# Padding each expert's rows to 64 instead of 128: 36 routed tiles in place of 39, the last four made of two experts' half tiles

## What is computed

```python
logits = x @ wg.T; probs = softmax(logits)            # 8 experts
top_w, top_idx = top_k(probs, 2); top_w /= sum(top_w) # two experts a row
for e in range(8):
    h = silu(x @ ex_gate[e].T) * (x @ ex_up[e].T)     # 256 -> 512
    out += h @ ex_down[e].T * comb[:, e:e+1]          # 512 -> 256
out += shared_mlp(x)                                  # the same form, every row
```

## Time and profile before

| | us |
|---|---|
| median of 3 runs | 375.55 (375.23 to 375.87) |
| profiled execution: span from first to last instruction | 371.5 |
| median less that span | 4.05 |
| TensorE matmul busy | 361.5 (97%) |
| VectorE busy | 280.9 (76%) |
| ScalarE busy | 217.7 (59%) |
| GpSimd busy | 197.4 (53%) |

### The profile page before, as it was taken

How to read it: one execution, slowest core, us unless ns; L and a number is a source line. 1 busy time by engine, 2 the same in 40 slices (tenths; PEclk the granted TensorE clock), 3 DMA queues, 4 the chain that set the end, 5 groups by cost and what they waited for, 6 DMA issues and landing times.

```text
span 371.5 us, 12942 instructions
## 1 busy us (share of the span) xinstructions
PE 361.5 (97%) x4978; PEld 314.9 (85%) x4983; DVE 280.9 (76%) x566; ACT 217.7 (59%) x457; POOL 197.4 (53%) x193
## 2 busy tenths in 40 slices
PE   8989998999999989999999999999999999999996
PEld 5546555788888879899999999999999999999995
DVE  6996388999999985679986887776778685555543
ACT  5688667687777855647357656565565634333222
POOL 2000003977888776122274687878677666674250
PEclk9999999999999999999999999999999999999999
DMA  7953031000198008989434465665757686665543
GB/s 262 379 78 48 2 131 41 2 4 30 41 380 151 30 31 311 347 305 250 109 91 90 112 114 91 106 111 87 118 99 94 106 104 89 104 113 76 71 58 114
DMA packets 53043, 45.35 MB, mean 122 GB/s; under 512 B 31524, under 2 KB 46996, under 8 KB 52856
## 3 DMA queue, kind: packets, MB, share of 16 engines
q1 hardware_dynamic: 43048, 32.09, 31.3%
q0 software_dynamic: 7488, 10.27, 19.0%
q10 hardware_dynamic: 2448, 2.18, 2.2%
HBM read 27.60 MB, written 10.49 MB: 103 GB/s over the span
## 4 chain that ended last, share of the span: by engine, by line
PE 69%; POOL 12%; DVE 7%; issue 5%; ACT 4%; DMA 1%; ACTq 0%; POOLq 0%; DVEq 0%
PE ps L1638 37%; PE ps L1656 18%; PE ps L1420 7%; POOL tmp L558 2%; POOL tmp L579 2%; PE ps L1406 2%; POOL tmp L562 2%; POOL tmp L577 2%; POOL wx L567 2%; POOL h2s L583 2%; DVE st L942 1%; DMA tmp<-in_decay_tables 1%; DVE tmp L959 1%; PE ps L1541 1%; ACT tmp L734 1%
## 5 line engine op out<-in xcount | busy, mean ns | idle before, releaser
L1638 PE MATMUL ps<-tmp,wx 128*128 128x128 bf16 x1776 | 105.5, 219 | 0.0
L1638 PEld LDWEIGHTS ps<-tmp,wx 128*128 (+1 forms) x1776 | 102.2, 98 | 0.9 <-issue 0.2
L615 POOL DMA_INDIRECT out<-tmp,dk x39 | 69.2, 1775 | 39.5 <-SPq L519 35.2
L862 ACT ACTIVATE tmp<-tmp 128x512 bf16<-128x512 f32 x55 | 34.6, 629 | 81.3 <-PE ps L1656 61.2
L1656 PE MATMUL ps<-wx,tmp 128*128 (+1 forms) x660 | 80.8, 273 | 0.2 <-DVE tmp L1267 0.2
L1656 PEld LDWEIGHTS ps<-wx,tmp 128*128 128x128 bf16 x660 | 62.2, 98 | 7.0 <-DVE tmp L1267 0.5
L1261 DVE TENSOR_TENSOR tmp<-ps,tmp 128x512 f32<-128x512 f32 x55 | 37.9, 689 | 36.0 <-PE ps L1638 31.3
L610 POOL DMA_INDIRECT tmp<-h2rows,src_i x39 | 43.5, 1116 | 16.7 <-issue 10.7
L1638 PE MATMUL ps<-w_hl,wx 128*128 128x128 bf16 x864 | 51.3, 219 | 0.5 <-ACT tmp L851 0.5
L1638 PEld LDWEIGHTS ps<-w_hl,wx 128*128 (+1 forms) x864 | 49.6, 98 | 1.1 <-issue 0.6
L1267 DVE TENSOR_TENSOR tmp<-tmp 128x512 bf16<-128x512 f32 x55 | 38.3, 696 | 10.7 <-ACT tmp L862 10.6
(11 more groups left out here) (196 smaller groups left out, 554.8 us busy)
## 6 DMA issues: line engine op xcount, KB each, us to landing
wx<-in_wexp SPq DMA_DIRECT2D x26, 512.0 KB, 5.2
xres<-in_x SPq DMA_DIRECT2D x4, 512.0 KB, 6.8
h2rows<-h2s ACTq DMA_DIRECT2D x16, 128.0 KB, 3.8
out<-h2s SPq DMA_DIRECT2D x12, 128.0 KB
h2s<-in_wmod SPq DMA_DIRECT2D x1, 1024.0 KB, 9.3
wx<-decay_rows SPq DMA_DIRECT2D x16, 64.0 KB
modr<-mod_rows SPq DMA_DIRECT2D x1, 1024.0 KB, 4.6
wx<-in_wqkvu SPq DMA_DIRECT2D x1, 768.0 KB, 7.0
```

What stands on the lines that cost most here:

```text
L615: e.indirect_dma_start(t["out"], bass.IndirectOffsetOnAxis(ap=dst_i[:, j:j + 1], axis=0), yb[(NA + j) % 2], None, compute_op=ALU.add).then ...
L862: e.activation(hs[p][:, 0:FF], hf[p], ACT.Copy).then_inc(s["inner_high"], 1)
L1638: ins = e.matmul(half(bank, m * P), weight(at_, weights(part, w) + k * FF + m * P, P), xT[f % NXT][:, (2 * a + k) * P:(2 * a + k + 1) * P] ...
```

## The change

- Each expert has as many full tiles of 128 as fit, plus one when over 64 rows are left; 1 to 64 left rows are a half. While fewer than 32 tiles are taken, a half gets a tile of its own; behind tile 32 two halves share one. So 32 full tiles are followed by 4 paired ones (PAIRS), 36 in all. The last paired tile has one half only.
- A paired tile makes gate and up with 64 moving columns for each half and its own expert's weights, and down once for each half, over all 128 stationary columns, into its own 256 columns of the bank. Its result is taken in two instructions of 64 partitions. It is added in two adds of 64 rows (the last in one): ADDS has 32 + 2 x 3 + 1 = 39 entries, as before.
- The adds of paired tiles are not asked of SyncE: GpSimd itself waits for the result and for both adds before.
- There are 4 result buffers (NY) in place of 2.
- The routing chain has 15 more links: 13 (with tiles_end, which moves forward) ahead of the marks, 2 more among those of iteration 8; a further instruction that is no link makes dst_upper. The weights' splits follow each other every 3 or 4 tiles instead of every 4.

```diff
+NFULL, NPAIR = TOP * NT, NE // 2
+NG = NFULL + NPAIR
-NG = TOP * NT + NE - 1
+PLACES = [*range(NG)]
+PAIRS = [j for j in range(NG) if PLACES[j] >= NFULL]
+ADDS = [(j, h) for j in range(NG) for h in ((0, 1) if j in PAIRS[:-1] else (0,) if j in PAIRS else (None,))]
+ASKED = [u for u in range(len(ADDS)) if ADDS[u][1] is None and (u == 0 or ADDS[u - 1][1] is None)]
+NY = 4
+SPLIT_FROM = (-1, 2, 6, 9, 13, 16, 20)
+        yb += [woutg[:].rearrange("p b k n -> p (b k n)")[:, (2 + i) * D:(3 + i) * D] for i in range(NY - 2)]
...
+        def halves(f):
+            return (0, 1) if f - NA in PAIRS[:-1] else (0,)
+        def experts_of(j):
+            return min(2 * PLACES[j] // 7 + 1, NE) if PLACES[j] < NFULL else NE
+        def added(eng, u):
+            wait(eng, s_added[u % 2], 16 * (u // 2 + 1) if u >= 0 else 0)
+        def last_add(j):
+            return max(u for u in range(len(ADDS)) if ADDS[u][0] == j) if j >= 0 else -1
...
-        PIECES_AT.update({NA - 1 + 4 * (x - 1) + q: ((x, q),) for x in range(1, NE) for q in range(NPIECE)})
-        ROUTING_AT = {4: 13, 5: 2, 6: 6, 7: 7, 8: 5, 9: 5, 10: 4, 11: 2}
+        PIECES_AT.update({NA + at_ + q: ((x + 1, q),) for x, at_ in enumerate(SPLIT_FROM) for q in range(NPIECE)})
+        ROUTING_AT = {4: 15, 5: 13, 6: 6, 7: 7, 8: 7, 9: 5, 10: 5, 11: 2}
...
             for f in range(NA + 6, NF):
-                if f - NA > 5:
-                    allow_add(f - NA - 6)
+                j = f - NA
+                while allowed < len(ASKED) and ADDS[ASKED[allowed]][0] <= (j - 6 if j - 6 < PAIRS[0] else j - 8):
+                    allow_add(ASKED[allowed])
+                    allowed += 1
                 turn_rows(f)
...
+            def add_rows(u):
+                j, h = ADDS[u]
+                if u in ASKED:
+                    e.wait_ge(s["may_add"], ASKED.index(u) + 1)
+                else:
+                    e.wait_ge(s["result_made"], j + 1)
+                    added(e, u - 2)
+                    added(e, u - 1)
+                rows = slice(0, P) if h is None else slice(h * HP2, (h + 1) * HP2)
+                to = dst_upper[0:HP2, j:j + 1] if h else dst_i[0:rows.stop, j:j + 1]
+                e.indirect_dma_start(t["out"], bass.IndirectOffsetOnAxis(ap=to, axis=0),
+                                     yb[j % NY][rows], None, compute_op=ALU.add).then_inc(s_added[u % 2], 16)
...
-                yield link(e.tensor_scalar(left, counts, float(P - 1), None, ALU.add))
+                yield link(e.tensor_scalar(left, counts, float(HP2 - 1), None, ALU.add))
                 yield link(e.tensor_scalar(tiles, left, -P, None, ALU.bitwise_and))
+                yield link(e.tensor_scalar(odd, left, HP2, HP2.bit_length() - 1, ALU.bitwise_and, ALU.logical_shift_right))
...
+                yield link(e.tensor_tensor(tiles_ahead, ahead, odd.unsqueeze(1).to_broadcast([P, NE, NE]), ALU.mult))
+                yield link(e.tensor_reduce(odd_at, tiles_ahead, AX.X, ALU.add))
+                yield link(e.tensor_reduce(total, tiles, AX.X, ALU.add))
+                yield link(e.tensor_scalar(cap, total, 0.5, float(NFULL * HP2), ALU.mult, ALU.add))
+                yield link(e.tensor_scalar(reach, odd_at, float(HP2), total, ALU.mult, ALU.add))
+                yield link(e.tensor_scalar(reach, reach, cap, total, ALU.min, ALU.max))
+                yield link(e.scalar_tensor_tensor(out=half_at, in0=odd_at, scalar=float(HP2), in1=reach, op0=ALU.mult, op1=ALU.add))
+                yield link(e.tensor_tensor(tiles_end, base, tiles, ALU.add))
+                yield link(e.tensor_tensor(jump, half_at, tiles_end, ALU.subtract))
+                ranks = half(FREE_BANK, 0, NT * NE).rearrange("p (t e) -> p t e", t=NT)
+                yield link(e.tensor_tensor(over, ranks, tiles.unsqueeze(1).to_broadcast([P, NT, NE]), ALU.is_ge))
+                yield link(e.tensor_tensor(over, over, jump.unsqueeze(1).to_broadcast([P, NT, NE]), ALU.mult))
+                yield link(e.tensor_tensor(pos, ranks, base.unsqueeze(1).to_broadcast([P, NT, NE]), ALU.add))
+                yield link(e.tensor_tensor(pos, pos, over, ALU.add))
...
-                    wait(e, s_added[j % 2], 16 * (j // 2))
+                    added(e, last_add(j - NY))
...
+                    for h in halves(f):
+                        rows = slice(h * HP2, (h + 1) * HP2) if paired(f) else slice(0, P)
+                        ins = e.scalar_tensor_tensor(out=yb[j % NY][rows], in0=ps[rows, DOWN_BANKS[f % 2], h * D:(h + 1) * D],
+                                                     scalar=slot_w[rows, j:j + 1], in1=gates[f % 2][rows], op0=ALU.mult, op1=ALU.mult)
+                    ins.then_inc(s["result_made"], 1)
...
+                for h in halves(f):
+                    e.reg_load(slot_reg, slot_of[0:1, 2 * j + h:2 * j + h + 1])
...
+                width = HP2 if paired(f) else P
+                for h, at_ in enumerate(homes):
+                    for m in range(KF):
+                        addresses(at_, [weights(part, w) + k * FF + m * P + LAST_COLUMN for k in range(KD) for w in range(2)])
+                        for n in range(3 * KD):
+                            k, (a, w) = n // 3, PASSES[n % 3]
+                            row = (2 * a + k) * P + h * HP2
+                            ins = e.matmul(half(bank, m * P + h * HP2, width), weight(at_, weights(part, w) + k * FF + m * P, P),
+                                           xT[f % NXT][:, row:row + width], start=n == 0, stop=n == 3 * KD - 1)
...
+                for h, at_ in enumerate(homes):
+                    for n in range(3 * KF):
...
+                        ins = e.matmul(half(DOWN_BANKS[p], h * D, D), hs[p][:, (KF * a + k) * P:(KF * a + k + 1) * P],
+                                       wx[:, off:off + D] if second else weight(at_, weights(2, w) + k * D, D),
+                                       start=n == 0, stop=n == 3 * KF - 1)
```

The two further links are in the chain that finds each half's expert:

```diff
+                yield link(e.scalar_tensor_tensor(out=odd_rank, in0=rank, scalar=-float(NE), in1=odd, op0=ALU.add, op1=ALU.mult))
                 yield link(e.tensor_scalar(passed, tiles_end, tile_col, None, ALU.is_le))
+                yield link(e.scalar_tensor_tensor(out=odd_rank, in0=half_at, scalar=tile_col, in1=odd_rank, op0=ALU.is_equal, op1=ALU.mult))
+                yield link(e.tensor_tensor(passed, passed, odd_rank, ALU.add))
```

More of the change, by code:

```diff
@@ L222, in build @@
         place_i, none_i, dst_i = (of_slots[:, i * NG:(i + 1) * NG].bitcast(u32) for i in range(2, 5))
+        dst_upper = of_slots[:, 5 * NG:6 * NG].bitcast(u32)
         tiles_end, base = (route(NE) for _ in range(2))
-        left, tiles = (route(NE, i32) for _ in range(2))
+        left, tiles, odd = (route(NE, i32) for _ in range(3))
+        odd_at, reach, half_at, jump, odd_rank, total, cap = (route(n) for n in (NE, NE, NE, NE, NE, 1, 1))
+        over = pick
         spare = at_tmp(5796, NG)
@@ L646, in _ @@
                 if j == 0:
-                    e.wait_ge(s["rows_found"], 2)
+                    e.wait_ge(s["rows_found"], 3)
                     e.wait_ge(s["x1_stored"], 16 * (B + 1))
                     e.wait_ge(s["base_stored"], 16 * NA)
-                add_rows(j)
+                for u in range(len(ADDS)):
+                    if ADDS[u][0] == j:
+                        add_rows(u)
         @block.scalar
@@ L1246, in routing @@
                 yield e.tensor_tensor(dst_i, none_i, src_i[:], ALU.add).then_inc(s["rows_found"], 1)
+                yield e.tensor_tensor(dst_upper[0:HP2], none_i[HP2:P], src_i[HP2:P], ALU.add).then_inc(s["rows_found"], 1)
                 yield link(e.tensor_scalar(batch, src_i[:], S, None, ALU.is_ge))
                 assert count[0] == RT_FLAGS
-                here, last = slot_of[:, 1:NG], slot_of[:, 0:NG - 1]
+                here, last = slot_of[:, 2:2 * NG:2], slot_of[:, 0:2 * NG - 2:2]
                 yield link(e.tensor_tensor(same_expert[:, 1:NG], here, last, ALU.is_equal))
@@ L1623, in gate_or_up @@
                 p = f % 2
-                at_ = slots_at[f] if routed(f) else SHARED_AT
+                homes = slots_at[f] if routed(f) else [SHARED_AT]
                 turned(e, f)
@@ L1632, in gate_or_up @@
                     j = f - NA
-                    e.wait_ge(s["expert_low"], NPIECE * min(j // FIRST_RANK + 1, NE) - (j == 0))
-                for m in range(KF):
-                    addresses(at_, [weights(part, w) + k * FF + m * P + LAST_COLUMN for k in range(KD) for w in range(2)])
-                    for n in range(3 * KD):
-                        k, (a, w) = n // 3, PASSES[n % 3]
-                        ins = e.matmul(half(bank, m * P), weight(at_, weights(part, w) + k * FF + m * P, P),
-                                       xT[f % NXT][:, (2 * a + k) * P:(2 * a + k + 1) * P],
-                                       start=n == 0, stop=n == 3 * KD - 1)
+                    e.wait_ge(s["expert_low"], NPIECE * experts_of(j) - (j == 0))
+                width = HP2 if paired(f) else P
```

(3 more changed lines are left out.)

57 lines of the change are left out of this document (25 added, 32 removed).

## The result

| | before | after |
|---|---|---|
| median of 4 runs, us | 375.71 (375.23 to 376.09) | 384.32 (383.35 to 385.72) |
| span of the profiled execution, us | 371.5 | 383.9 |
| TensorE matmul busy, us | 361.5 | 357.0 |

After to before: 1.0227, 95% interval 1.0181 to 1.0273. The change makes the kernel slower by 8.6 us; the forecast was 1.4 faster.

What follows compares the result with a forecast made beforehand. TensorE, busy for 97% of the span, was taken to bound the kernel. 4.4 us gained at the end less 3.0 lost in routing made 1.4 off 375.55: 374.2 us, range 371.0 to 378.2.

Steps and rivals of the forecast that it cites:

- rival (b): Last adds: half adds cost nearly what whole ones do, so their series makes the kernel slower, 377.0 to 380.5; chance 0.31.
- the price of a half add, 3.1 us: Seven serial adds at the end: each takes 3.1 us against 4.0 for a whole one; bounds 2.7 and 4.0.
- Result 32, 16.1 behind the start of tile 32: First paired tile's result, from which the serial half adds begin: ready 16.1 us after gate and up of routed tile 32.
- The tail of 7.4: Behind the last half add's landing: two loads, three sums, the end of the span and hand-overs, 7.4 us.
- 4.4 gained: End of the kernel, set by the serial half adds: 45.2 us after tile 32's start in place of 49.6.
- The routing chain, 3.0: Routing stage: 13 more VectorE links ahead of the marks delay TensorE before tile 12, 3.0 us lost; bounds 2.4 and 3.9.
- TensorE alone, 7.5: End of the kernel: 7.5 us gained if TensorE's work alone set the end, without the wait for adds.
- The 31 ns of the 64-column matmul: Paired tiles' gate and up on TensorE: each narrow matmul takes 31 ns; bounds 27 and 55.8.
- rival (d): Paired tiles: narrow matmuls run no faster than wide ones, 55.8 ns, so 4.8 us lost, 380.4; chance 0.03.
- Cost nothing: Additional buffers, denser weight splits, SyncE's queue, gathers and additional takings of a result: no time added.
- the cover of one step: Weight splits: each piece is issued a step before the tile that needs it, so TensorE need not stand idle.

Runs made afterwards that it cites:

- the run of links alone: The kernel before with thirteen more links in the routing chain ahead of the marks, results unused, nothing else of the change: 376.91 us, ratio 1.0097.
- the second set: Follow-up kernels run together on one chip where TensorE ran without stillness; the kernel before took 373.71 us there.
- The controls: The changed kernel, with SyncE keeping an asked add's loaded number from falling below nought, run on two chips: 385.57 us, ratio 1.0214; 384.69 us, ratio 1.0173.

## Why the prediction was wrong

The side was wrong, and the time outside the range. It was rival (b) that came, with its mechanism and at its upper price: a half add 4.0 us from start to start. It had 0.31. Its time, 380.5, is 3.8 short as well, for the reasons below that stand beside the price.

- **The step that failed: the price of a half add, 3.1 us.** In flight it is 3.03 to 3.41 and not 2.83 (GpSimd's part falls from 1.55 to 1.42, not to 1.16; it has hardly a part by rows). And the hand-over is 0.77 from the landing, 0.71 of it behind the waiting instruction, and not 0.27: I took it from an add whose one wait stands in its instruction, while the change waits for two forerunners and a result. Its own diff showed three waits. The 4.0 stood there as a half add that saves nothing; it came as a saving of 0.6 in flight eaten by 0.5 more of hand-over. From result 32 to the last landing 27.4 us stand against 7 x 3.1 = 21.7: 5.7 us.
- **Result 32, 16.1 behind the start of tile 32: it was 17.5.** Zero is here, as in the forecast, the start in the chain: 331.24, and the result is there at 348.74. The register loads behind narrow matmuls are 1.94 us and not 0.9 (0.91 and 0.71 for the two loads, and 0.32 where one load was to fit): 1.0. The other 0.4 are matmul groups that took longer than summed (a narrow one of 3.19 us, a down of 1.63).
- **The tail of 7.4 was 7.7.** With it the end is 52.7 behind zero and not 45.2: 7.4 us missed in this part, and in place of 4.4 gained 3.0 lost (49.6 before).
- **The routing chain, 3.0: right in place and mechanism, 0.4 to 0.6 short.** 3.4 in the run of links alone, 3.6 in the changed kernel's trace. Down 5 waits 1.67 and down 6 1.14, both for L1331; and 0.3 more stand ahead of gate and up of tile 12.
- **TensorE alone, 7.5: nearly right.** In the second set from the product at 206.69 to that at 361.04 are 154.4 us, in the kernel before 161.3 (203.18 to 364.49): 7.0 gained. The 31 ns of the 64-column matmul were exact; rival (d) is out.
- **"Cost nothing":** right for result buffers and gathers at the places of the change. The denser splits cost nothing on a chip where TensorE ran without stillness, and 2 to 3 us on the two others where it was tried; that the cover of one step could be too little there, the forecast didn't see.

The sum of the terms with their measured sizes: 3.0 lost at the end and 3.5 in the routing stage, 6.5 us or 1.7%. The controls have 1.7% and 2.1%. The remaining 2 us of the changed kernel's 8.6 fit the dense pieces on a chip with stillness (2 to 3 us there), but no run took that apart on the chip of the first comparison.

(b) leaned on the Trainium skill, "DMA: Bandwidth & Descriptors", section "Anatomy of one DMA — SWDGE (gpsimd) path": a fixed time that is most of an add. The fall of 0.1 from 64 to 32 rows agrees; the fall of 0.8 from 128 to 64 is more than its bytes account for (an estimated 0.15 by that section). The 3.85 for a half add, estimated from it, would have given 379.4.

## What to carry to other kernels

Splitting a transfer in two where each part must wait for the one before pays the fixed part twice. Price a serial one as landing plus hand-over, and count the waits that its instruction must hold: only one is cheap. Ask of a series not how long it is but what runs beside it: with the same adds four places earlier (and two smaller edits) the kernel was level with the old one. And before a difference between two traces is given to the change, see where each traced execution lies against its median, and look for the difference in a second trace of the old kernel on the same chip. Measure such stretches on the engine that bounds them: between two products of VectorE the control's middle looked 1.0 us shorter than the old kernel's, between TensorE's starts it is 1.5 longer, because VectorE was late at the first mark.

## What was not expected of the hardware

- A wait in an instruction of its own ahead of a GpSimd DMA makes 0.77 us of the 0.27 from a landing to the next start.
- A serial add of 32, 64 and 128 rows of 1 KB comes every 3.91, 3.99 and 4.78 us (the 64 on other chips): the step lies between 64 and 128.
- On three of five chips TensorE stood still for 0.2 to 0.6 us at a time inside runs of matmuls, at full granted clock; on the one where both kernels were traced, in both. The kernel before took 376.3 to 378.8 us on these chips against 373.7 and 374.0 on the other two; where it was traced, its middle was 4.3 us longer than in the first trace (132.2 against 127.8). It differs between executions too: on one of the three chips the kernel with 32 rows an add needed 128.7 us for the middle, that with 128 rows 131.8. Its cause stays open.
